# Local attention in a fused kernel: probabilities divided ahead of their transposes, the values product made transposed, the inverse lengths by Ln and Exp

## What is computed

```
x = x + attn_a(layernorm(x))   # a mamba block beside two plain projections
x = x + ffn(layernorm(x))      # two transformer layers
x = x + attn_b(layernorm(x))   # attention with a distance decay
x = x + ffn(layernorm(x))      # the same two transformer layers, called again
```

```
qkv = shift_token(x) @ wqkv;  q, k, v = split(qkv)     # 128 -> 3 x 512
q = l2norm(q) * q_scale; k = l2norm(k) * k_scale       # per head
q, k = rotary_xpos(q, k)
# a query sees its own window and the one before it, at most 64 back
attn = softmax(where(mask, -big, (q * 8) @ k^T))
x = x + (attn @ v) @ wo                                # 512 -> 128
x = x + ffn_gelu(layernorm(shift_token(x)))
```

## Time and profile before

| | |
|---|---|
| median of 3 runs | 2251.19 us (2249.34 to 2251.57) |
| profiled execution, its own time | 2245.52 us |
| its span, first to last instruction | 2243.7 us |
| TensorE busy | 2140.1 us, 95% |
| VectorE busy | 1613.2 us, 72% |
| ScalarE busy | 1475.8 us, 66% |
| GpSimd busy | 1677.2 us, 75% |
| mean granted TensorE clock | 0.992 |

### The profile page before, as it was taken

One profiled execution on the slowest core, in us unless ns is written; L12 is line 12 of the kernel. 1 busy time (PEld: TensorE's weight loads), 2 busy tenths in 40 slices (PEclk: granted clock), 3 DMA queues, 4 the chain that ended last, 5 costly groups with the idle time before them and its releaser, 6 DMA issues.

```text
span 2243.7 us, 54540 instructions
## 1 busy us (share of the span) xinstructions
PE 2140.1 (95%) x19744; PEld 1477.6 (66%) x19760; DVE 1613.2 (72%) x3907; ACT 1475.8 (66%) x4130; POOL 1677.2 (75%) x1710
## 2 busy tenths in 40 slices
PE   6999889999999999899999999999999989999998
PEld 4767657777567777556666666565777756777765
DVE  6777568887467777667767777777888756777765
ACT  3666458888458888536656556566888854888862
POOL 7877788998158888448777787778898824888852
PEclk9999989999999999999999999999999999999999
DMA  4000001112111122121111121111111211111211
GB/s 118 1 1 1 7 21 44 35 32 49 48 29 40 33 46 46 43 71 50 49 54 35 48 58 50 44 27 23 42 25 44 46 45 31 37 34 40 47 31 51
DMA packets 121371, 88.42 MB, mean 39 GB/s; under 512 B 85560, under 2 KB 102160, under 8 KB 118800
## 3 DMA queue, kind: packets, MB, share of 16 engines
q1 hardware_dynamic: 118544, 82.69, 15.2%
q10 hardware_dynamic: 2560, 2.24, 0.4%
HBM read 30.38 MB, written 8.39 MB: 17 GB/s over the span
## 4 chain that ended last, share of the span: by engine, by line
PE 65%; DVE 7%; POOL 5%; SPq 5%; issue 3%; DMA 2%; ACT 1%; POOLq 0%; DVEq 0%
PE bank L1328 11%; PE bank L593 8%; PE bank L1339 5%; PE bank L1319 5%; PE bank L607 5%; PE bank L654 4%; PE bank L642 4%; PE bank L629 4%; PE bank L600 4%; PE bank L668 4%; SPq L466 4%; POOL store L1140 3%; PE bank L720 2%; PE bank L662 2%; POOL store L1149 2%
## 5 line engine op out<-in xcount | busy, mean ns | idle before, releaser
L1552 POOL TENSOR_SCALAR store<-store 128x512 f32<-128x512 f32 x512 | 348.7, 693 | 108.2 <-DVE store L1479 106.7
L1479 DVE CUSTOM_DVE_ANT_0 store<-bank,store 128x512 f32<-128x512 f32 x512 | 335.7, 689 | 119.2 <-PE bank L1319 66.8
L1435 ACT ACTIVATE store<-bank 128x512 f32<-128x512 f32 x512 | 286.7, 600 | 201.3 <-PE bank L1328 197.8
L844 ACT ACTIVATE store<-bank,store 128x128 f32<-128x128 f32 x1024 | 362.6, 375 | 69.5 <-DVE store L987 69.4
L1134 POOL TENSOR_TENSOR store<-store 128x512 f32<-128x512 f32 x256 | 320.9, 1275 | 105.7 <-DVE store L974 101.1
L1140 POOL TENSOR_TENSOR store<-store 128x16 f32<-128x16 f32 x128 | 372.5, 2911 | 27.8 <-DVE store L983 27.4
L1328 PEld LDWEIGHTS bank<-store 128*128 128x128 f32 x2048 | 239.7, 141 | 133.1 <-ACT store L1435 75.8
L1328 PE MATMUL bank<-store 128*128 128x128 f32 x2048 | 297.9, 277 | 0.1
L1149 POOL TENSOR_TENSOR store<-store 128x512 f32<-128x512 f32 x256 | 261.5, 1042 | 10.0
L593 PE MATMUL bank<-store 128*128 128x512 f32 x496 | 253.5, 597 | 0.0
L987 DVE TENSOR_REDUCE store<-bank 128x4 f32<-128x512 f32 x256 | 165.0, 686 | 122.9 <-PE bank L629 122.8
(11 more groups left out here) (220 smaller groups left out, 4442.8 us busy)
## 6 DMA issues: line engine op xcount, KB each, us to landing
store<-store SPq DMA_DIRECT2D x256, 128.0 KB, 2.4
store<-parts SPq DMA_DIRECT2D x96, 192.0 KB
parts<-store SPq DMA_DIRECT2D x16, 384.0 KB, 3.6
store<-store SPq DMA_DIRECT2D x128, 32.0 KB
store<-store SPq DMA_DIRECT2D x128, 31.8 KB
store<-store SPq DMA_DIRECT2D x32, 127.0 KB
store<-in_L_ffn_wqkv_dram SPq DMA_DIRECT2D x4, 768.0 KB, 4.3
out_dram<-store SPq DMA_DIRECT2D x8, 256.0 KB, 2.4
```

The costliest lines, as they stand in the source:

```text
L844: last = nc.scalar.activation(prob[:, e, b, :], bank[3 + e][:, b * P:(b + 1) * P], ACT.Exp, bias=nmax[:, e, b:b + 1], accum_out=psums[:, h ...
L1435: nc.scalar.activation(AT[:, h % 4, c, :], bank[SCORE_BANKS + (64 * q + 4 * h + c) % TURN_BANKS][:, :], ACT.Exp, scale=-1.0).then_inc(aexp ...
L1479: nc.vector.tensor_tensor_reduce(out=S[:, h % 4, t, :], in0=bank[(64 * q + 4 * h + t) % SCORE_BANKS][:, :], in1=decay[:, off:off + L], sca ...
L1552: nc.gpsimd.tensor_scalar(s_, s_, -1.0, amax[:, h % 4, t:t + 1], ALU.mult, ALU.add).then_inc(shifted_done, 1)
```

## The change

- The sums are kept and inverted per half. The probabilities are multiplied by the inverse sums before they are transposed: half 0 on GpSimd, half 1 on VectorE (`scale_probs`). `take_o` is gone.
- `weigh_values` holds the values fixed and streams the transposed probabilities, so that its result is already transposed; `o_transpose` is gone, and `copy_oT` follows the product directly.
- The second half's transposes of tile j-1, and their copy, move into step j; the output projection and its addition move to two tiles later. Both halves of `project_qk` move ahead of `weigh_values`, and `qk_transpose` behind it.
- The inverse lengths are exp(-0.5 ln(.)) on ScalarE in place of the power on GpSimd, and the table set that holds both functions is loaded ahead of each entry.

```diff
 TensorE, attention_sequence:
                     scores(q, j, ff_ahead and j == 0)
                     if has_prev:
-                        weigh_values(*prev)
+                        prob_transpose(*prev, 1, True)
+                    if has_prev2:
+                        project_out(*prev2)
                     if more or j < 2:
                         project_v(*((q, j + 2) if j < 2 else (q + 1, j - 2)), more or j == 0)
+                    if has_ahead:
+                        project_qk(*ahead, 0)
+                        project_qk(*ahead, 1)
+                    if has_prev:
+                        weigh_values(*prev)
                     if has_next:
                         qk_transpose(*nxt)
-                    if has_prev:
-                        o_transpose(*prev)
                     prob_transpose(q, j, 0, has_next)
-                    if has_ahead:
-                        project_qk(*ahead, 0)
-                    if has_prev:
-                        project_out(*prev)
-                    if has_ahead:
-                        project_qk(*ahead, 1)
-                    prob_transpose(q, j, 1, has_next)
                     if more:
                         x_transpose(q + 1, j, False)
 weigh_values:
-                            last = nc.tensor.matmul(bank[7][half * WIN:(half + 1) * WIN, h * DH:(h + 1) * DH],
-                                                    probT[:, e, b, half * WIN:(half + 1) * WIN], v[:, j, h * DH:(h + 1) * DH],
+                            last = nc.tensor.matmul(bank[7][e * DH:(e + 1) * DH, b * P + half * WIN:b * P + (half + 1) * WIN],
+                                                    v[:, j, h * DH:(h + 1) * DH], probT[:, e, b, half * WIN:(half + 1) * WIN],
 prob_transpose:
-                pe.wait_ge(exp_done, n2 + e + 3)
+                pe.wait_ge(scaled_p[e], 4 * q + j + 1)
 ScalarE, attention_sequence:
                     exps(q, j, 0)
-                    if more or j < 2:
-                        copy_v(*ahead)
-                    if more or j < 3:
-                        copy_qkT(*((q, j + 1) if j < 3 else (q + 1, 0)))
-                    if before or j:
-                        copy_oT(*((q, j - 1) if j else (q - 1, TPS - 1)))
+                    if has_prev:
+                        copy_pT(*prev, 1)
                     exps(q, j, 1)
+                    if has_prev:
+                        copy_oT(*prev)
+                    if more or j < 3:
+                        copy_qkT(*((q, j + 1) if j < 3 else (q + 1, 0)))
+                    if more or j < 2:
+                        copy_v(*ahead)
                     copy_pT(q, j, 0)
-                    copy_pT(q, j, 1)
+                    if more or j < 2:
+                        inverse_lengths(act, *ahead)
 VectorE, attention_sequence:
                     maxima(q, j, 0)
                     maxima(q, j, 1)
-                    if has_prev:
-                        take_o(*prev)
+                    if before or j > 1:
+                        add_out(s if j > 1 else s - 1, *((q, j - 2) if j > 1 else (q - 1, j + 2)))
                     if more or j < 2:
                         ahead = (q, j + 2) if j < 2 else (q + 1, j - 2)
                         rotate(*ahead, 0)
+                    inverse_sums(q, j, 0)
+                    if more or j < 2:
                         rotate(*ahead, 1)
                         square_sums(*ahead)
-                    inverse_sums(q, j)
-                    if has_prev:
-                        add_out(s if j else s - 1, *prev)
+                    inverse_sums(q, j, 1)
+                    scale_probs(q, j, 1)
 GpSimd:
+            def scale_probs(q, j):
+                pool.wait_ge(pinv_done[0], 4 * q + j + 1)
+                nc.gpsimd.tensor_tensor(prob[:, 0, :, :], prob[:, 0, :, :], bc(pinv[:, 0, :], 2, P), ALU.mult).then_inc(scaled_p[0], 1)
...
+                    scale_probs(q, j)
                     if more or j < 2:
                         finish_qk(*((q, j + 2) if j < 2 else (q + 1, j - 2)))   # without inverse_norms
 ScalarE, new:
+        def inverse_lengths(act, q, j):
+            flat = norm[:, 2 * (j % 2):2 * (j % 2) + 2, :].rearrange("p i h -> p (i h)")
+            act.wait_ge(clip_done, 4 * q + j + 1)
+            nc.scalar.activation(flat, flat, ACT.Ln).then_inc(log_done, 1)
+            act.wait_ge(log_done, 4 * q + j + 1)
+            nc.scalar.activation(flat, flat, ACT.Exp, scale=-0.5).then_inc(norm_done, 1)
```

More of the change, by code:

```diff
@@ L194, in hybrid_block @@
         probT = mem.take(2, PAIRS, P)
-        onorm = mem.take(INNER)
         oT = mem.take(PAIRS, P)
         nmax = mem.take(2, PAIRS)
-        psums = mem.take(H)
-        pinv = mem.take(H)
+        psums = mem.take(2, PAIRS)
+        pinv = mem.take(2, PAIRS)
         fq = mem.take(2, TPS, P)
@@ L291, in hybrid_block @@
         sim_done, max_done, exp_done = sem("sim_done"), sem("max_done"), sem("exp_done")
-        pT_done, pT_ready, o_done, onorm_ready = sem("pT_done"), sem("pT_ready"), sem("o_done"), sem("onorm_ready")
-        oT_done, oT_ready = sem("oT_done"), sem("oT_ready")
+        pT_done, pT_ready, o_done, oT_ready = sem("pT_done"), sem("pT_ready"), sem("o_done"), sem("oT_ready")
+        pinv_done, scaled_p = [sem("pinv_done0"), sem("pinv_done1")], [sem("scaled_p0"), sem("scaled_p1")]
         va_in = [sem(f"va_in{i}") for i in range(SLOTS)]
@@ L648, in weigh_values @@
                 pe.wait_ge(va_in[j], (32 if j < TPS - 1 else 16) * (q + 1))
[L649 to L653, removed]
-                            last = nc.tensor.matmul(bank[7][half * WIN:(half + 1) * WIN, h * DH:(h + 1) * DH],
-                                                    probT[:, e, b, half * WIN:(half + 1) * WIN], v[:, j, h * DH:(h + 1) * DH],
+                pe.wait_ge(pT_ready, n2 + 2)
+                for b in range(PAIRS):
+                    for half, v in ((0, VA), (1, V)):
+                        for e in range(2):
+                            h = 2 * b + e
+                            last = nc.tensor.matmul(bank[7][e * DH:(e + 1) * DH, b * P + half * WIN:b * P + (half + 1) * WIN],
+                                                    v[:, j, h * DH:(h + 1) * DH], probT[:, e, b, half * WIN:(half + 1) * WIN],
                                                     start=True, stop=True, skip_group_check=True)
                 last.then_inc(o_done, 1)
[L659 to L663, removed]
             def project_out(q, j):
@@ L674, in attention_sequence @@
                     prev = (q, j - 1) if j else (q - 1, TPS - 1)
-                    has_prev = before or j > 0
+                    prev2 = (q, j - 2) if j > 1 else (q - 1, j + 2)
+                    has_prev, has_prev2 = before or j > 0, before or j > 1
                     nxt = (q, j + 1) if j < 3 else (q + 1, 0)
@@ L803, in transformer_pe @@
                 attention_sequence(q0 + (B - 1), True, False)
+                prob_transpose(q0 + (B - 1), TPS - 1, 1, False)
                 ff_normed(q0, True)
+                project_out(q0 + (B - 1), TPS - 2)
                 weigh_values(q0 + (B - 1), TPS - 1)
@@ L853, in copy_oT @@
             def copy_oT(q, j):
-                act.wait_ge(oT_done, 4 * q + j + 1)
+                act.wait_ge(o_done, 4 * q + j + SLOTS + 1)
                 nc.scalar.activation(oT[:, :, :].rearrange("p b t -> p (b t)"), bank[7][:, :], ACT.Copy).then_inc(oT_ready, 1)
@@ L858, in attention_sequence @@
                 for j in range(TPS):
+                    prev, has_prev = (q, j - 1) if j else (q - 1, TPS - 1), before or j > 0
                     if more or j < 2:
@@ L904, in ff_rounds @@
                 if new:
+                    nc.scalar.preload_act_table_set("natural_log_exp_and_others")
+                    inverse_lengths(act, q1, 0)
                     squares(q1, 1)
@@ L907, in ff_rounds @@
                     copy_qkT(q1, 0)
+                    inverse_lengths(act, q1, 1)
             for l in range(DEPTH):
@@ L917, in transformer_act @@
                 act.wait_ge(ff_w, (l + (call * DEPTH + 1)) * (16 * FF_LOADS))
+                copy_pT(q0 + (B - 1), TPS - 1, 1)
                 ff_affine(q0, 0)
@@ L988, in maxima, with inverse_sums, scale_probs @@
                                         AX.X, ALU.max, negate=True).then_inc(max_done, 1)
[L990 to L1000, removed]
+            def inverse_sums(q, j, e):
+                dve.wait_ge(exp_done, 8 * q + 2 * j + e + 3)
+                nc.vector.reciprocal(pinv[:, e, :], psums[:, e, :]).then_inc(pinv_done[e], 1)
+            def scale_probs(q, j, e):
+                dve.wait_ge(pinv_done[e], 4 * q + j + 1)
+                nc.vector.tensor_tensor(prob[:, e, :, :], prob[:, e, :, :], bc(pinv[:, e, :], 2, P), ALU.mult).then_inc(scaled_p[e], 1)
             def add_out(s, q, j):
@@ L1012, in attention_sequence @@
                         ff_normalize(ff_from, 0, ff_from == 0)
-                    has_prev = before or j > 0
```

(17 more changed lines are left out.)

15 lines of the change are left out of this document (4 added, 11 removed).

## The result

The changed kernel takes 2457.88 us (median of 4 runs, 2456.4 to 2460.0), the kernel before beside it 2250.27 us. The ratio is 1.0928, 95% interval 1.0911 to 1.0945: 207.6 us slower. Forecast were 2430 us and +180. The profiled execution took 2460.0 us around a span of 2458.2, so 214.5 more by either measure.

The account below looks back on a forecast made before the run. TensorE was taken as the bound, with 65% of the chain. Layers of 307.0 us against 260.6 and 263.6 add +46.4 and +43.4, twice each: +180 us, edges 0, giving 2430 us; range 2350 to 2480 at 80%.

Parts of the forecast that it names:

- Two stalls in series: Per tile, TensorE waits for VectorE's rotations, then for ScalarE's v copy; the step becomes 10.2 us against 8.41.
- Scores to q/k projection: First part of a step: rotations start at 3.00 and end at 5.60, holding the second q/k projection half until 5.65.
- q/k projection to the next scores: Second part: values product at 6.65, ScalarE copies until 9.95, x transpose at 10.00, next scores at 10.20.
- What hides what: In a full step, other ScalarE, GpSimd and VectorE work, including the added multiplies and functions, makes nothing else later.
- Size of a full step: One tile in the middle of a sequence takes 10.2 us from scores to scores, with an error of some 0.25 us.
- The other steps: Steps at a layer's start and last sequence, from 7.0 to 9.74 us; with 26 full ones, 307.0 us a layer.
- next scores at 7.0 each: Last sequence's second and third steps, without q/k projection, take 7.0 us each, 14.0 together.
- What bounds the kernel before: TensorE holds 65% of the chain, and nothing another engine delivers is late on the tile shown.
- rival 3: TensorE's clock falls to the 1.2 GHz level: at most +500 us, 2480 if one tile in ten; 8%.
- Edges: Entering and leaving layers, plus one possible table load: taken as 0, kept at -12 to +13 us.
- Rival 4: Ln and Exp from different table sets force switches each tile: +2.2 us a tile, 2710 us; 3%.
- Rivals 1 and 2: TensorE stays the bound, steps 8.0, 2189 us, 5%; or only the first stall occurs, steps 9.5, 2357 us, 8%.

Follow-up runs that it names:

- Edit two: The changed kernel with both project_qk calls moved back behind the values product and q/k transposes on TensorE: 2268.01 us, 1.0099.
- edit one: The changed kernel with copy_v moved back ahead of the second exponentials on ScalarE: 2400.03 us, 1.0681.
- the extra multiply: The changed kernel plus one unused 128x512 VectorE multiply: ahead of the rotations 2529.15 us, at the end of VectorE's step 2468.88 us.
- nine: The changed kernel without the clip on VectorE, the logarithm adding 1e-24 instead: 2454.64 us, 1.0913.
- eight: The kernel before with only the inverse lengths changed, Ln and Exp on ScalarE replacing GpSimd's power: 2228.28 us, 0.9908.
- four: The changed kernel with project_qk late, v copy early, second probability copy ahead of the first exponentials, and the clip as a two-tensor instruction: 2255.14 us, 1.0037.
- five: The changed kernel with project_qk late, second probability copy first, v copy last, no clip, and normalization right behind add_out: 2185.89 us, 0.9723.
- eleven: The changed kernel with project_qk late, v copy early, second probability copy first, plus normalization moved right behind add_out: 2237.96 us, 0.9945.

## Why the prediction was right

The walk against the trace, in us from the scores' start:

| step | forecast | measured |
|---|---|---|
| rotations start | 3.00 | 3.00 (419.95) |
| last rotation ends, TensorE goes on | 5.60, 5.65 | 5.55, 5.60 (422.55) |
| values product | 6.65 | 6.66 (423.61 in the timeline) |
| output copy | 7.84 | 7.85 (424.80) |
| q, k, v copy | 8.36, 8.86, 9.35 | 8.43, 8.92, 9.40 |
| x transpose | 10.00 | 10.15 (427.10) |
| next scores | 10.20 | 10.38 |

- *Two stalls in series* (steps "Scores to q/k projection" and "q/k projection to the next scores"): right. Edit two takes away the first and with it 190 us, edit one the last copy of the second and 58; the extra multiply shows that VectorE's stretch is on the route.
- *What hides what*: right. GpSimd's multiply, Ln and Exp, and the second VectorE multiply are not on the chain of a full step. ScalarE was idle 2.42 us before the output copy (forecast: some 2.4). But VectorE's clip was not 0.26 but 1.27 us long, which I had not foreseen. In the full steps there was room.
- *Size of a full step*: 0.18 us short, 18.9 us over 104 steps. Restarting TensorE on a copy took 0.14 us before the matmul (426.96 to 427.10), where I had 0.05; the q copy came 0.07 later than the transposes' 0.60 let me expect.
- *The other steps*: "next scores at 7.0 each" is the term that failed: the third step of the last sequence took 8.66 us in two layers and 9.94 in two, 9.2 us in sum. I had left out what else VectorE does in it, which is in its list: the feed-forward statistics (L1043, L1048) stand ahead of the maxima, and the multiply behind the clip ahead of them. The clip, held by GpSimd, stands ahead of both; taking it out (nine) shortened these steps by 0.3 us where the clock was the same. The maxima started 2.75 us after the scores instead of 1.33:

```profile
1013.61 1.27 DVE L990 TENSOR_SCALAR store<-store 128x16 f32<-128x16 f32 x1
1014.80 0.16 DVE L999 RECIPROCAL store<-store 128x4 f32<-128x4 f32 x1
1014.99 0.69 DVE L1003 TENSOR_TENSOR store<-store 128x512 f32<-128x512 f32 x1
1015.61 0.86 DVE L1043 BATCH_NORM_STATS2 store<-store 128x6 f32<-128x128 f32 x4
1016.61 0.38 DVE L1048 BATCH_NORM_AGGREGATE store<-store 128x2 f32<-128x6 f32 x4
1016.91 1.26 DVE L994 TENSOR_REDUCE store<-bank 128x4 f32<-128x512 f32 x2
```

- *What bounds the kernel before*: "nothing another engine delivers is late" holds for the tile shown, not for all: with the power gone from GpSimd (eight) the steps of 8.5 and 9.03 us fell to 8.41.
- *The clock* (rival 3): it kept 1.00 in the full steps (windows view below), where TensorE waits 0.81, 0.34 and 0.35 us. In the layers' steps it fell only where TensorE had waited 2.45 us or 1.62: in two of the third steps, 1.28 us each, and in the first layer's first step, 10.26 instead of 8.66. By the Trainium skill, "TensorE: Matmul & The Clock Gate", "What's actually happening", idleness returns the engine to its throttled state; these rows agree (0.50 after the stall), though the same waits in the other layers left 1.00:

```profile
663.00:1006.00 343.00, 296.44 (x3026) 185.78 (x3024) 244.97 (x437) 226.62 (x776) 173.23 (x161) 1.00 0.14 32
...
613.00:616.00 3.00, 0.81 (x8) 0.61 (x6) 1.93 (x8) 1.88 (x10) 1.19 (x3) 0.98 0.00 0
616.00:618.00 2.00, 1.75 (x32) 1.78 (x32) 0.43 (x2) 1.50 (x9) 1.92 (x3) 0.50 0.00 0
```

- *Sum*: steps 1228 forecast and 1261 measured, 33 short: 18.9 in full steps, 9.2 in third steps, 1.7 in the first layer's first step, 3.2 in the rest. *Edges* 0 forecast, 2.4 measured. Then 180 + 33 + 2 = 215, the 214.5 of the profiles.
- *Rival 4*: no table load inside a tile. From the first attention step on, the trace has eight loads, none of them between the first and the last scores of a layer.
- *Rivals 1 and 2* did not hold: steps were neither 8.0 nor 9.5.

## What to carry to other kernels

Where engines meet only at semaphores, the order of each engine's list is the schedule. Moving a consumer ahead of work that needs nothing turns hidden producers into a round trip, and then the saved matmuls are worth nothing: 0.44 us less work, 1.97 us longer steps. Before such a move, put the release time of every wait beside the time at which the engine would now reach it; the rows of one tile are enough. And look at a change's parts singly: here Ln and Exp alone were worth -20 us, and the whole, with the order mended, the clip taken out and the normalization moved, -63 instead of +208.

## What the runs showed of the hardware

**GpSimd's instructions hold some of VectorE's.** The clip of 16 columns, from the source view of the kernel before (L983) and of the changed one (L990), duration ns min/median/max:

```profile
L983 DVE TENSOR_SCALAR store<-store x124: 174/263/855, 309.1 to 2149.5; 128x16 f32<-128x16 f32 x124
```

```profile
L990 DVE TENSOR_SCALAR store<-store x124: 175/1273/1282, 309.6 to 2361.2; 128x16 f32<-128x16 f32 x124
```

It ends with GpSimd's addition in the changed kernel (1014.88 against 1014.85 in the second layer's third step):

```profile
1012.35 2.50 POOL L1136 TENSOR_TENSOR store<-store 128x512 f32<-128x512 f32 x2
```

Held were instructions that read only SBUF, in the form of tensor and number (clip, normalization) and in that of two tensors (four's clip, nine's multiply, the latter 1.72 for 0.69 us). Not held were the reduction (1.21 us), those with an operand in PSUM (0.68), and, reading only SBUF too, the reciprocal (at 1007.36 in nine, 0.17) and the feed-forward statistics (at 1015.61, 0.86). A multiply that had begun before GpSimd's next instruction kept its 0.69 (1014.99 against 1015.45). Taking one held instruction out passed the hold to the next such one (nine, five). The Trainium skill, "GPSIMD Engine Reference", "Key points", says that the two engines share SBUF interfaces and contend over VectorE's instructions with two SBUF inputs or in a two-port mode; the rows with two SBUF inputs agree, and they give the size: up to the rest of GpSimd's instruction, 1.0 us here. In which mode the tensor-and-number form ran no row shows. Such an instruction is better put where GpSimd is idle: moved there, two normalizing instructions went from 2.07 to 0.60 us, and the kernel became 16 us faster (eleven).

**TensorE's clock over short stalls.** Behind 2.45 us without work the product kept its 1.15 us in the second layer and took 1.97 in the first (at 616.25); through the gaps of under 1 us in the full steps the clock stayed at 1.00 (windows view, 663 to 1006, above).

```profile
1019.74 1.15 PE L660 MATMUL bank<-store 128*64 128x64 f32 x32 [2.45 <-ACT store L849]
```

So a stall of this length may or may not bring the lower clock, and one kernel shows both.
